# Products of a delta rule ahead of its scan: from one chunk of 32 tokens to blocks of two chunks, with another order of filters and batches

## The reference, cut to what matters

```python
# per batch b, head h, chunk n: q, k, v are [32 tokens, 32 channels]; beta is one number a token
v, k_beta = v * beta, k * beta
A = k_beta @ k.T
T = inv(eye + tril(A, -1))            # 32 x 32, unit lower triangular
u, w = T @ v, T @ k_beta
def body(S, (q, k, u, w)):            # a scan over the 32 chunks
    attn = where(tri, q @ k.T, 0)
    u = u - w @ S
    o = q @ S + attn @ u
    return S + k.T @ u, o
local_short = causal_dwconv(v, fir_short)      # 3 taps
local_long  = causal_dwconv(v, fir_long)       # 31 taps
o = w_global * o + (1 - w_global) * (p0 * v + p1 * local_short + p2 * local_long)
```

## Time and profile before

| | us |
|---|---|
| median of 3 runs | 634.15 (633.8 to 635.01) |
| the profiled execution | 636.29 |
| its span, first to last instruction | 634.5 |
| filters and their transposes, to the first product | 425.94 to 469.99 |
| the eight products | 469.99 to 529.04 |
| scan to the end | 529.04 to 634.5 |

### The profile page before, as it was taken

One profiled execution on the slowest core, in us unless ns is written; L12 is line 12 of the kernel. 1 busy time (PEld: TensorE's weight loads), 2 busy tenths in 40 slices (PEclk: granted clock), 3 DMA queues, 4 the chain that ended last, 5 costly groups with the idle time before them and its releaser, 6 DMA issues.

```text
span 634.5 us, 19355 instructions
## 1 busy us (share of the span) xinstructions
PE 546.9 (86%) x8432; PEld 379.9 (60%) x8432; DVE 399.9 (63%) x769; ACT 310.0 (49%) x563; POOL 175.9 (28%) x332
## 2 busy tenths in 40 slices
PE   4799999999999999898989999969984546788993
PEld 2445555555555567676777876747863535566772
DVE  5697999998999462534435364467993312466674
ACT  3227878878888764646454565530051010124441
POOL 7001112354544330000000032269894300010201
PEclk9799999999999999999999999978986655568998
DMA  3778675554320000010000000213033000000011
GB/s 112 161 220 220 172 155 113 103 117 81 74 53 4 4 2 0 1 35 1 1 1 1 1 0 2 35 39 67 4 69 70 4 4 4 6 1 1 1 34 33
DMA packets 37450, 31.83 MB, mean 50 GB/s; under 512 B 22245, under 2 KB 28901, under 8 KB 37366
## 3 DMA queue, kind: packets, MB, share of 16 engines
q1 hardware_dynamic: 36374, 30.08, 20.8%
q10 hardware_dynamic: 992, 0.53, 0.4%
HBM read 20.83 MB, written 9.44 MB: 48 GB/s over the span
## 4 chain that ended last, share of the span: by engine, by line
PE 67%; DVE 11%; DMA 7%; ACT 7%; issue 5%; SPq 1%; POOL 1%; POOLq 0%; DVEq 0%; ACTq 0%
PE ps L1644 9%; PE ps L1629 8%; PE ps L1410 6%; PE ps L1745 6%; PE ps L1412 6%; PE ps L1411 6%; DMA qst<-shift_sb 5%; PE ps L1608 2%; PE ps L1773 2%; PE ps L1904 2%; PE ps L1905 2%; PE ps L1853 2%; PE ps L1801 2%; ACT prob L628 2%; DVE hf L978 2%
## 5 line engine op out<-in xcount | busy, mean ns | idle before, releaser
L1110 DVE TENSOR_REDUCE nmx<-ps 128x1 f32<-128x1024 f32 x128 | 154.1, 1218 | 16.9 <-PE ps L1609 15.6
L628 ACT ACTIVATE prob<-ps 128x512 f32<-128x512 f32 x256 | 137.5, 597 | 27.7 <-PE ps L1629 26.9
L1644 PE MATMUL ps<-prob,vp 128*32 128x128 f32 x2048 | 78.9, 278 | 0.0
L1629 PE MATMUL ps<-qst,kst 50*128 50x512 f32 x256 | 73.6, 492 | 5.5 <-ACT prob L628 3.4
L1644 PEld LDWEIGHTS ps<-prob,vp 128*32 128x32 f32 x2048 | 49.1, 109 | 39.7 <-ACT prob L628 22.4
L983 DVE TENSOR_TENSOR h_lo<-hf,h_hi 128x512 fp32r<-128x512 f32 x48 | 33.1, 691 | 58.0 <-ACT h_hi L537 57.6
L1410 PE MATMUL ps<-h_hi,w_lo 128*128 128x512 f32 x144 | 59.1, 410 | 2.5 <-DVE h_lo L983 2.1
L1412 PE MATMUL ps<-h_hi,w_hi 128*128 128x512 f32 x144 | 56.8, 395 | 0.0
L1411 PE MATMUL ps<-h_lo,w_hi 128*128 128x512 f32 x144 | 56.8, 395 | 0.0
L1608 PE MATMUL ps<-kst,qst 48*128 48x512 f32 x128 | 52.7, 413 | 1.4 <-DMA kst<-k_scratch 0.8
L1609 PE MATMUL ps<-kst,qst 48*128 48x512 f32 x128 | 51.4, 403 | 0.0
(11 more groups left out here) (237 smaller groups left out, 1097.4 us busy)
## 6 DMA issues: line engine op xcount, KB each, us to landing
qst<-q_scratch SPq DMA_DIRECT2D x31, 192.0 KB, 4.6
kst<-k_scratch SPq DMA_DIRECT2D x31, 192.0 KB, 4.9
w_raw<-L_ffn_h_w SPq DMA_DIRECT2D x8, 256.0 KB, 3.6
X<-L_attn_x SPq DMA_DIRECT2D x4, 256.0 KB, 5.1
qst<-shift_sb SPq DMA_DIRECT2D x64, 4.0 KB
q_scratch<-w_hi SPq DMA_DIRECT2D x2, 512.0 KB, 5.2
k_scratch<-w_lo SPq DMA_DIRECT2D x2, 512.0 KB, 3.1
low_dram<-low SPq DMA_DIRECT2D x8, 128.0 KB, 2.9
```

Of the source, the lines that this page charges most:

```text
L628: nc.scalar.activation(prob[:, n % PROBS, GT * (t % 2):GT * (t % 2) + GT], ps[:, RINGB + i % RING, :], ACT.Exp, scale=SCORE_SCALE).then_in ...
L1110: nc.vector.tensor_reduce(nmx[:, u % 2, j:j + 1], pair, AX.X, ALU.max, negate=True).then_inc(max_done, 1)
L1629: nc.tensor.matmul(ps[:, RINGB + i % RING, :], kst[r:r + 50, p, P * t:P * t + P], half_of(qst[r:r + 50, p, :], u % 2), start=True, stop=Tr ...
L1644: last = nc.tensor.matmul(ps[32 * j:32 * j + 32, PVB, P * half:P * half + P], vp[:, h, t, :], prob[:, n % PROBS, c:c + P], start=(t == 0), ...
```

## The change

- **Blocks of two chunks.** `tT` becomes two tiles of [128, 32, 64] (one a batch), zeroed by POOL, in which the inverses of chunks 2p and 2p+1 stand on the diagonal of a 64x64 block. A new tile `kd` ([128, 8, 4, 2, 2, 32] a batch) holds [k, triangle] in the same way: for chunk c only the half c % 2 of the last-but-one axis is filled, by DMA from `ka`, the rest is zero (batch 0 zeroed by ACT, batch 1 by POOL once the filters are done). Products 1, 3 and 4 become 64 calls for a pair of chunks in place of 128; product 2 stays at 128 calls.
- **Order on PE.** The 3-tap filter first (banks 0 to 3), then 8 of the 31 taps (banks 4 to 7), the 3-tap transposes, the other 23 taps. Then: product 1 of batch 0, transposes of the long filter, product 2 of batch 0, product 3 of batch 0 (banks 4 to 7), product 1 of batch 1, product 4 of batch 0, products 2, 3 and 4 of batch 1 (product 3 in banks 0 to 3).
- **Order elsewhere.** ACT's copies follow that order. SP issues, for each batch, four `kd` loads before the store of the inverse, and the load of `tT` is four DMAs. POOL's `sw1` and `sw2` move behind the first two of the four filter additions and behind product 4 of batch 0.

Tiles and banks:

```diff
-    tT = sb4("tT", [P, B, C, C])
+    tT0 = sb4("tT0", [P, 32, 2 * C])
...
+    tT1 = sb_blocks("tT1", [P, 32, 2 * C])
+    kd0 = sb_blocks("kd0", [P, 8, 4, 2, 2, C])
+    kd1 = sb_blocks("kd1", [P, 8, 4, 2, 2, C])
...
+    FIR_BANK, MG_BANK = (4, 0), (4, 0)
```

The program of SP:

```diff
+            sp.wait_ge(tT_zeroed, 1)
             for b in range(B):
+                sp.wait_ge(kd_zeroed[b], 1)
+                sp.wait_ge(ktok_ready, 2 * b + 2)
+                sp.wait_ge(att_ready, 2 * b + 2)
+                for c in range(4):
+                    r = slice(32 * c, 32 * c + 32)
+                    sp.dma_start(kd[b][r, :, :, :, c % 2, :], ka[r, 8 * b:8 * b + 8]).then_inc(kd_in[b], 16)
                 sp.wait_ge(inv_ready[b], 1)
                 sp.dma_start(inv_dram[b].rearrange("h n c e i -> (h n c) e i"), tp[:, b]).then_inc(inv_stored[b], 16)
                 sp.wait_ge(inv_stored[b], 16)
-                sp.dma_start(tT[:, b], inv_dram[b].rearrange("h n c e i -> (c e) (h n) i")).then_inc(inv_in[b], 16)
+                for c in range(4):
+                    r = slice(32 * c, 32 * c + 32)
+                    sp.dma_start(tT[b][r, :, C * (c % 2):C * (c % 2) + C], inv_dram[b].rearrange("h n c e i -> c e (h n) i")[c]).then_inc(inv_in[b], 16)
```

The program of ACT:

```diff
+            act.wait_ge(tT_zeroed, 1)
+            nc.scalar.copy(kd0[:].rearrange("p n h a d e -> p (n h a d e)"), zero[:].broadcast_to([P, 32 * 4 * C])).then_inc(kd_zeroed[0], 1)
...
+            copy_filtered(1)
+            copy_filtered_tokens(1)
+            copy_filtered(0)
+            copy_uw(0)
+            copy_filtered_tokens(0)
+            copy_b(0)
+            copy_uw(1)
+            copy_b(1)
```

The program of POOL:

```diff
-            link(nc.gpsimd.memset(state[:, 0], 0.0))
+            link(nc.gpsimd.memset(zero[:], 0.0))
+            link(nc.gpsimd.memset(tT0[:], 0.0))
+            nc.gpsimd.memset(tT1[:], 0.0).then_inc(tT_zeroed, 1)
             start_inverse(nc.gpsimd, link, 0)
...
-            pool.wait_ge(conv_psum, 3 * GROUPS)
-            for k in range(FB):
-                last = nc.gpsimd.tensor_scalar(sw1[:, k, :], k1[:, k, :], s_twice[:, 0:1], s_sign[:, 1:2], ALU.mult, ALU.subtract)
-            last.then_inc(signs_ready, 1)
-            nc.gpsimd.tensor_scalar(sw2, k2[:], 2.0, -1.0, ALU.mult, ALU.add).then_inc(signs_ready, 1)
+            pool.wait_ge(fir_psum, 2)
+            nc.gpsimd.memset(kd1[:], 0.0).then_inc(kd_zeroed[1], 1)
...
             for i, g in enumerate(FINAL):
+                if i == 2:
+                    pool.wait_ge(uw_psum, B)
+                    nc.gpsimd.memset(state[:, 0], 0.0).then_inc(state_zeroed, 1)
+                    pool.wait_ge(o_begun, 1)
+                    for k in range(FB):
+                        last = nc.gpsimd.tensor_scalar(sw1[:, k, :], k1[:, k, :], s_twice[:, 0:1], s_sign[:, 1:2], ALU.mult, ALU.subtract)
+                    last.then_inc(signs_ready, 1)
+                    nc.gpsimd.tensor_scalar(sw2, k2[:], 2.0, -1.0, ALU.mult, ALU.add).then_inc(signs_ready, 1)
```

The program of PE:

```diff
-            filter_values(0)
+            filter_values(1, range(FIRS)).then_inc(fir_psum, 1)
             pe.wait_ge(att_ready, GROUPS)
-            filter_values(1)
-            filtered_to_tokens(0)
+            filter_values(0, range(8))
             filtered_to_tokens(1)
+            filter_values(0, range(8, FIRL)).then_inc(fir_psum, 1)
...
+            def times_inverse(b):
+                pe.wait_ge(inv_in[b], 4 * 16)
+                pe.wait_ge(vb_ready[b], 2)
+                pe.wait_ge(kb_ready[b], 2)
+                for n in range(8):
+                    for h in range(4):
+                        for p in range(2):
+                            r = pair(p)
+                            last = nc.tensor.matmul(ps[r, n // 2, (4 * (n % 2) + h) * 64:(4 * (n % 2) + h) * 64 + 64], tT[b][r, 8 * h + n, :],
+                                                    vk[r, 8 * b + n, h].rearrange("p a e -> p (a e)"), start=True, stop=True)
+            def transition_products(b):
+                pe.wait_ge(kd_in[b], 4 * 16)
+                for n in range(8):
+                    for p in range(2):
+                        r = pair(p)
+                        for h in range(4):
+                            last = nc.tensor.matmul(ps[32 * h:32 * h + 32, MG_BANK[b] + 2 * p + n // 4, 4 * C * (n % 4):4 * C * (n % 4) + 4 * C],
+                                                    uw(b, r, n, h)[:, 32:64], kd[b][r, n, h].rearrange("p a d e -> p (a d e)"), start=True, stop=True)
             def begin_outputs(b):
                 for n in range(8):
                     for h in range(4):
-                        for c in range(4):
-                            r = slice(32 * c, 32 * c + 32)
-                            last = nc.tensor.matmul(o_region(b, n, c, h), ka[r, 8 * b + n, h, 1, :], uw(b, r, n, h)[:, 0:32],
+                        bank, cols = o_place(b, n, h)
+                        for p in range(2):
+                            r = pair(p)
+                            last = nc.tensor.matmul(ps[r, bank, cols], kd[b][r, n, h, 1].rearrange("p d e -> p (d e)"), uw(b, r, n, h)[:, 0:32],
...
+            pe.wait_ge(fir_tok_ready, 4)
+            times_inverse(0)
+            filtered_to_tokens(0)
+            inputs_of_state(0)
             pe.wait_ge(fir_tok_ready, 8)
+            transition_products(0)
+            pe.wait_ge(b_ready, 1)
+            times_inverse(1)
+            pe.wait_ge(m_ready, 1)
+            pe.wait_ge(g_ready, 1)
+            begin_outputs(0)
+            inputs_of_state(1)
+            pe.wait_ge(b_ready, 2)
+            transition_products(1)
+            begin_outputs(1)
             pe.wait_ge(o_begun, B)
+            pe.wait_ge(state_zeroed, 1)
```

More of the change, by code:

```diff
@@ L223, in program, with sb_blocks @@
     sub.close()
+    blocks = ExitStack()
+    def sb_blocks(name, shape, dt=F32):
+        return blocks.enter_context(nc.sbuf_tensor(name, shape, dt))
+    sb_blocks("below_state", [P, LIVE + 6 * C * C + 2 * C * C + TAPS * C + 2 * C * C])
+    tT1 = sb_blocks("tT1", [P, 32, 2 * C])
+    sb_blocks("below_x", [P, B * C + 4 * S + 4 * S + 4 * S + 2 * S + GT])
+    kd0 = sb_blocks("kd0", [P, 8, 4, 2, 2, C])
+    sb_blocks("below_v", [P, 4 * XCOLS - 4 * S])
+    kd1 = sb_blocks("kd1", [P, 8, 4, 2, 2, C])
+    blocks.close()
+    tT, kd = (tT0, tT1), (kd0, kd1)
     last_stage = ExitStack()
@@ L672, in _, with copy_filtered, copy_filtered_tokens, copy_uw @@
             ktok_copy(GROUPS - 1)
-            for k in range(2):
-                act.wait_ge(fir_psum, k + 1)
+            act.wait_ge(tT_zeroed, 1)
+            nc.scalar.copy(kd0[:].rearrange("p n h a d e -> p (n h a d e)"), zero[:].broadcast_to([P, 32 * 4 * C])).then_inc(kd_zeroed[0], 1)
+            def copy_filtered(k):
+                act.wait_ge(fir_psum, 2 - k)
                 for h in range(4):
-                    nc.scalar.copy(filtered[:, k, h, :], ps[:, 4 * k + h, :]).then_inc(fir_copied, 1)
-            for k in range(2):
+                    nc.scalar.copy(filtered[:, k, h, :], ps[:, FIR_BANK[k] + h, :]).then_inc(fir_copied, 1)
+            def copy_filtered_tokens(k):
                 for h in range(4):
-                    act.wait_ge(fir_tok_psum, 4 * k + h + 1)
-                    nc.scalar.copy(filtered[:, k, h, :], ps[:, 4 * k + h, :]).then_inc(fir_tok_ready, 1)
-            for b in range(B):
+                    act.wait_ge(fir_tok_psum, 4 * (1 - k) + h + 1)
+                    nc.scalar.copy(filtered[:, k, h, :], ps[:, FIR_BANK[k] + h, :]).then_inc(fir_tok_ready, 1)
+            def copy_uw(b):
                 act.wait_ge(uw_psum, b + 1)
@@ L1736, in _, with filter_values @@
             k_to_tokens(GROUPS - 1)
-            def filter_values(k):
-                for t in range((FIRL, FIRS)[k]):
+            def filter_values(k, taps):
+                for t in taps:
                     for i in range(16):
@@ new lines, in times_inverse @@
+            def times_inverse(b):
[8 more added lines that the diff above has]
+                                                    vk[r, 8 * b + n, h].rearrange("p a e -> p (a e)"), start=True, stop=True)
+                last.then_inc(uw_psum, 1)
@@ L1768, in per_chunk, with inputs_of_state @@
+            def inputs_of_state(b):
+                pe.wait_ge(uw_ready, b + 1)
                 for n in range(8):
                     for i in range(16):
-                            c, h = i % 4, (i + i // 4) % 4
-                            r = slice(32 * c, 32 * c + 32)
-                            bank, o = place(n, c)
-                            last = nc.tensor.matmul(ps[32 * h:32 * h + 32, bank, o:o + cols], lhs(r, n, h), rhs(r, n, h), start=True, stop=True)
-                return last
@@ L1776, in o_region @@
-            def o_region(b, n, c, h):
+                        c, h = i % 4, (i + i // 4) % 4
+                        r = slice(32 * c, 32 * c + 32)
```

(6 more changed lines are left out.)

56 lines of the change are left out of this document (21 added, 35 removed).

## The result

The changed kernel takes 624.75 us (median of 4, 622.68 to 625.3), the kernel before, measured beside it, 633.97; the ratio is 0.9846, with a 95% interval of [0.982, 0.9871]. The forecast was 620.6 with a range of 613 to 628. The profiled execution after took 624.37 with a span of 622.6, where before it was 636.29 and 634.5.

The account below looks back on a forecast made before the run. PE was taken as bound by instruction fetch, 3.69 us per packet of 128 records. Start 468.3 + 36.9 fetch + 3.2 + 3.5 + 0.6 + 1.9 + 0.6 + 0.5 = 515.5, 13.5 us less: median 620.6 us, range 613 to 628.

Parts of the forecast that it names:

- Fewer records: Between first product and scan, 1280 records in 10 packets at 3.69 us take 36.9 us, where it was 59.05.
- nothing is won: Rival: idle time belongs to each product, not each packet, so it stays; about 634 us; chance 0.03.
- pieces on the same rows do not overlap: Slower rival: in product 3 each load waits for the running multiply of its rows; 662 us; chance 0.06 for slower.
- The sum: First product at 468.3, plus fetches and extras, puts the scan's start at 515.5 in place of 529.04, 13.5 us less.
- Product 1: 64x64 blocks take 5.3 us a batch, between 4.2 and 6.7; 3.2 us over two fetches.
- Product 4: 64-column weight loads make it 4.4 us for batch 0, 6.5 for batch 1; 3.5 us over two fetches.
- Product 3: In eight pieces it takes 4.0 us a batch, between 2.5 and 4.9; 0.6 us over two fetches.
- Product 2: Keeps 256 records a batch, two packets, 7.4 us; expected to stay about 7 us.
- The waits on ACT and on the inverse of batch 1: PE waits ahead of batch 1's products: 0.6 us for ACT's copies (0 to 1.3), 0.5 for the inverse (0 to 1.9).
- What I cost at nothing: POOL's 3.8 us clearing of `tT` ahead of its inverse lies in its 5.87 us wait for tokens, costing nothing.
- the signs that it named for itself: 10 or 11 packets; product 1 at 4 to 7 us, product 2 7, batch 1's product 4 about 6; scan near 515.
- three against itself: PE waiting over 3 us for `tT1`, a product 3 over 5 us, or a scan that grows.

Follow-up runs that it names:

- the last kernel: D with POOL's weighting of the values by the mix waiting for DVE's inverse of batch 1; 609.16 us, ratio 0.9588.
- D: C with the five small clearings of its mask also moved to POOL's wait ahead of its inverse; 610.59 us, ratio 0.9613.
- C: Changed kernel with `tT` clearings moved to POOL's wait, batch 1's `kd` loads after its inverse's, and product 2 in 64 two-chunk calls a batch; 611.95 us.
- no alternation: Changed kernel with `tT` clearings moved to POOL's wait and product 4 of batch 0 ahead of product 1 of batch 1; 627.11 us, ratio 0.9858.
- all narrow: Changed kernel with `tT` clearings moved to POOL's wait and products 1, 3 and 4 back in 128 one-chunk calls a batch; 635.64 us, ratio 0.9994.
- product 1 narrow: Changed kernel with only product 1 cut back into 32x32 pieces, 128 calls a batch in place of 64; 624.68 us, ratio 0.9837.

## Why the prediction was right, and where it failed

*Fewer records.* This was right, and it is shown from both sides: 16 packets with the new order take 59.65 us, and two packets more for product 2 take 7.2 us more in that product. The trace of the kernel before also shows what the 3.69 us consist of. Here are two bursts of its product 3, and what the DMA view has from 487.0 to 488.5 us (from 484.5 to 487.0 and from 488.5 to 490.8 it has no packet at all):

```profile
486.00 1.95 PE L1773 MATMUL ps<-ka,inv_flat 32*32 32x64 f32 x128 [0.87 <-issue]
489.73 1.67 PE L1773 MATMUL ps<-ka,inv_flat 32*32 32x64 f32 x105 [1.77 <-issue]
```

```profile
q8 instruction: 1, 0.02, 5.4%
```

The packet sets out at 487.1, about 1.1 us after PE began on the first burst. It takes 1.3 us (5.4% of 16 engines in 1.5 us), and PE's next burst begins 1.3 us after that. These three parts make the 3.7 us: here one packet follows another, and there are not two on the way. The new transfers of `kd` do not slow the packets; by the shares they took 1.05 us each after and 1.18 before, an estimate.

The rivals "nothing is won" and "pieces on the same rows do not overlap" fell: 128 records of product 3 took 3.83 us, mostly at the lower clock, in the last kernel and 2.10 at the upper one in D.

*The sum.* From the filters to the first product 42.1 us came where 42.4 was forecast; from there to the scan 46.7 where 47.2 was. That the second agrees is luck: terms that were together about 5.5 us too low meet terms about 6 us too high. Product 1 took 6.64 and 6.19 in place of 5.3, the first mostly at the lower clock; at the upper one it took 3.95 (C, no alternation), so the two bounds, 6.7 and 4.2, were near and the value between them too low. Product 4 likewise: 3.88 at a clock of 1.00, 7.04 at 0.50, where the two bounds were 3.2 and 6.5; batch 1's was charged with 6.5 and took 4.57. Product 3 took 5.5 and 4.7 in place of 4.0, for it lay at the lower clock (4.3 us of work each) and carries waits for instructions. Product 2 was charged with 7.4 and took 6.3 and 4.9: while product 1, the transposes and product 4 run, a packet comes in ahead of its use, and the packets do not simply follow one another at 3.69 us, as the sum had it. The waits on ACT and on the inverse of batch 1 stood where they were put, with 1.3 and 0.8 us in place of 0.6 and 0.5. (The moment at which PE wants that inverse, 487.1, was added up with 4.2 for product 3 where the sum has 4.0.)

*What I cost at nothing: POOL's clearing of `tT`.* This step failed. The clearings did lie in POOL's wait for tokens, so POOL itself lost nothing; but between them and that wait stands `fir_diag`, and it moved onto DVE's work. The cost was 4.25 us in the stage ahead of the filters (55.12 to 59.37). It is nearly the whole distance between the forecast and the time, 624.75 - 620.6 = 4.15; without the clearings there the kernel takes 618.4, which lies 2.2 below the forecast.

What DVE waits for is seen in the rows after: the operation of 128x32 took 1.77 us from 373.91 and ended at 375.68, just as POOL's clearing of 373.84 + 1.80 = 375.64 did; the four of the normalisation ended at 379.23, just behind `fir_diag` at 378.84. Before, the same operation took 1.30 us and ended with `fir_diag`, which stood there then (375.48 and 375.44); in C, where it began just ahead of `fir_diag`, it took 0.18. So part of this wait was there before, and what the change added is mostly the normalisation's.

The Trainium skill, "SBUF — State Buffer", SBUF: two separate sides, calls the port pair that GpSimd and DVE share an exclusive lock: between a GpSimd operation and a DVE operation that is in a two-port mode, or that has two SBUF inputs while the GpSimd operation reads SBUF, the one that starts first holds the pair for its whole length and the other blocks. The trace agrees with these ends, though no row names the mode of an operation. It agrees with DVE's inverse too, whose steps have two inputs: one takes 1.02 us beside POOL's products, which read, and 0.28 without, and the step of 0.37 us beside POOL's clearing of `kd1`, which reads nothing, is no longer than its neighbour of 0.39 ahead of the clearing.

*The range* of 613 to 628 held the time. Of the signs that it named for itself, 10 packets and product 1's length came; product 2 at 7 us, product 4 of batch 1 at 6 and a scan near 515 (it starts at 518.68) did not. Of the three against itself, a wait over 3 us for `tT1` and a longer scan did not come; product 3 of batch 0 did pass 5 us, by 1.26 us of wait inside it and a clock of 0.50. What cost the most lay in a stage that the sum had set as constant.

*Open.* Why the granted clock is at one level or the other inside the products was not tried by itself; it moves products 1 and 4 by some 3 us each from one kernel's execution to another's. A wait alone does not tell: ahead of product 1 of batch 0 PE waited 2.93 us in the kernel after and 3.12 without alternation, and ran it mostly at 0.50 in the one and at 1.00 in the other. Nor was it settled why the scan's stage after is 1.5 us shorter.

## What to carry to other kernels

Where PE issues many small products, count its instructions and the packets in which they come (256 to a packet here): blocks are worth what they save in fetch, and only where the fetch does not get ahead anyway. A step that "lies in a wait" of its engine also moves what stands between it and that wait: look at what each moved operation lands beside on the other engines, POOL beside DVE above all. And where PE stands idle longer than before, read the granted clock behind the gap, and price both.

## What was not expected of the hardware

A delay of POOL by 0.75 us cost 1.7 us at the filters, and one of 3.6 us cost 4.3: in these two the loss came by where POOL's operation fell on DVE's, not by the length of the delay, and more than half of it came behind, where the clock was at the lower level. Product 4 with 64 columns of weights ran at 30 ns a record at a clock of 1.00 and 55 at 0.50, product 1 at 31 and, mostly at the lower level (0.55), at 52. After the filters PE ran 165 records of a narrow product 1 before it stopped inside it (all narrow, and product 1 narrow alike): little more than one packet was there ahead.
